# Attention: identity and causal masks of the mask products in float32r instead of bf16

## The chip, the cores and the metric

The kernel runs on one core of a Trainium2 chip. The core has a matrix engine (TensorE, PE in the rows), VectorE (DVE), ScalarE (ACT), GpSimd (POOL) and a queue of DMA issues (SyncE, SP). They run side by side and wait for each other by semaphores. The metric is the device time of one execution in microseconds (us), lower is better. A matrix product reads its two operands from the on-chip memory SBUF and adds up its result in PSUM. It has two parts: a weight load, which puts one operand into the array, and the matmul proper, which streams the columns of the other operand through it.

## What is computed

The reference is a transformer block with adaptive layer norm. The part that the change touches is a causal attention with 16 heads of 16 channels over 8 batches of 1024 tokens:

```python
h = _layernorm(x, axis=-1) * (1 + ca) + sa
att = jnp.einsum('bhtd,bhsd->bhts', q, k) * scale
causal = jnp.tril(jnp.ones((T, T), dtype=bool))
att = jnp.where(causal[None, None, :, :], att, -jnp.inf)
att = jax.nn.softmax(att, axis=-1)
y = jnp.einsum('bhts,bhsd->bhtd', att, v)
x = x + ga * (y @ Wp + bp)
```

Here q, k and v are projections of h. Behind it follow two layers of windowed attention and a gated MLP (another stage of the program), which the change leaves alone.

## The kernel before

Three stages follow each other: a small one for the modulation rows, the attention stage (`attention_stage`), and the layers' stage. Each begins when the one before has ended. The attention stage goes through the 8 batches ("turns"), and in each through 4 groups of 4 heads. A group is 12 steps (`STEPS1`): a step is one block of 128 keys against up to 512 queries. The instructions of each engine are written out in this order by Python loops; nothing reorders them afterwards.

Each group needs the scores twice. `first_pass` (L882) computes them with queries on the partitions, only for the row maxima, which VectorE takes (L1050). It makes 24 units of up to 512 keys for each group, two in each step. `scores` (L907) computes them with keys on the partitions and the maxima subtracted by two extra rows; ScalarE takes the exponentials from there (L728), and `meet_values` (L924) multiplies these by the values. Both kinds of scores handle a pair of heads at once: one head uses rows 0 to 63 of the array (48 or 50 of them), the other rows 64 to 127, each writing its own half of a PSUM slot of 1024 columns. There are three such slots (`a_ring`), filled in turn; a fill waits until ScalarE or VectorE has read the slot. Operands of the scores are float32r (the name `f32` in the rows covers both float32 and float32r).

Where a block lies on the diagonal, the forbidden pairs of query and key must be masked. `add_mask` does it with further products: the transposed "identity" picks 64 rows of a mask, and the product adds -1e30 to the forbidden scores in PSUM. The mask of 128 x 128 is made in two parts of 64 rows each, and each part is done for both heads, so one masked block takes four matmuls and four weight loads of 64 rows by 128 columns. With `mask_ts` (first pass) the two parts stream 128 and 64 columns, with `mask_st` (scores) 64 and 128. The mask matmuls belong to the same accumulation as the scores, and the last of them releases the slot to its reader.

In a group 16 of the 24 units and 16 of the 24 score blocks are masked. In these a block has 128, 256, 384 or 512 columns, each equally often. Over 32 groups that is 512 masked blocks of each kind.

The constants are made by GpSimd at the start of the stage: memsets to zero, then `affine_select`, which writes the fill value where a condition on row and column fails. A count on `const_made` orders them; TensorE and VectorE wait for its last value.

Of the kernel before, what the change touches and what calls it, by code (L numbers as in the profile page):

```python
# [18 lines left out]
F32R = mybir.dt.float32r  # L19
BF16 = mybir.dt.bfloat16  # L20
# [5 lines left out]
P = 128  # L26
# [105 lines left out]
class Chain(Signal):  # L132
# [5 lines left out]
    def step(self, ins):  # L138
        self.seen += 1
        ins.then_inc(self.sem, 1)  # L140
        self.eng.wait_ge(self.sem, self.at(self.i, self.seen))
# [208 lines left out]
def attention_stage(nc, sems, x_in, w_in, b_in, mod_dram, x1_dram, f_dram, parts_unused, max_unused, turns):  # L350

    with ExitStack() as ctx:
        sb = lambda name, shape, dt=F32: ctx.enter_context(nc.sbuf_tensor(name, shape, dt))
# [11 lines left out]
        b_p = sb("a_b_p", [P, C])  # L365
        gate_bp = sb("a_gate_bp", [P, 1, C])
        ident = sb("a_ident", [P, P])
        ident_h = sb("a_ident_h", [P, 2, P], BF16)
        mask_ts = sb("a_mask_ts", [P, 2, P], BF16)
        mask_st = sb("a_mask_st", [P, 2, P], BF16)  # L370
        mod_in = sb("a_mod_in", [P, 2, C])
        modb = sb("a_modb", [P, NMOD - 3, C])
        xl = sb("a_xl", [P, TB, C])
# [28 lines left out]
        const_made = plain("a_const_made")  # L402
# [198 lines left out]
        @block.gpsimd  # L601
        def _(pool):
            pool.memset(ident[:, :], 0.0).then_inc(const_made, 1)
            pool.memset(ident_h[:, :, :], 0.0).then_inc(const_made, 1)
            pool.memset(mask_ts[:, :, :], 0.0).then_inc(const_made, 1)
            pool.memset(mask_st[:, :, :], 0.0).then_inc(const_made, 1)
            pool.memset(v_t[:, :, :, D1:VW], 0.0).then_inc(const_made, 1)
            pool.wait_ge(const_made, 5)
            pool.memset(v_t[:, :, :, D1:D1 + 1], 1.0).then_inc(const_made, 1)
            pool.memset(mx[:, :, :, :, :, :], MASKED).then_inc(const_made, 1)  # L610
            for r in range(2):
                pool.wait_ge(const_made, 7 + r)
                pool.memset(k_st[64 * r + 32:64 * r + 64, :, :].bitcast(F32), -1.0).then_inc(const_made, 1)
            pool.wait_ge(const_made, 9)
            pool.affine_select(out=ident[:, :], in_=ident[:, :], compare_op=ALU.not_equal, fill=1.0, base=0,
                               pattern=[[-1, P]], channel_multiplier=1).then_inc(const_made, 1)

            for r in range(2):
                rows = slice(64 * r, 64 * r + 64)
                for m, op, fill, sign in ((ident_h, ALU.not_equal, 1.0, 1), (mask_ts, ALU.is_ge, MASKED, 1),  # L620
                                          (mask_st, ALU.is_ge, MASKED, -1)):
                    pool.wait_ge(const_made, 10 + 3 * r + (0 if m is ident_h else 1 if m is mask_ts else 2))
                    pool.affine_select(out=m[rows, :, :], in_=m[rows, :, :], compare_op=op, fill=fill, base=0,
                                       pattern=[[64 * sign, 2], [-sign, P]], channel_multiplier=sign)\
                        .then_inc(const_made, 1)
            pool.wait_ge(w_loaded, 16 * (NW + 4))

            def modulate(dst, src, name, shift, scale, scaling, scaled, done, a):

                aggr, rstd = norms[name]["aggr"], norms[name]["rstd"]  # L630
                pool.wait_ge(rstd_of[name].sem, rstd_of[name].at(a, 1))
                pool.sem_inc(scaling.sem, 1)
                for t in range(TB):
                    ins = pool.tensor_scalar(dst[:, t, :], src[:, t, :], aggr[:, t, 0:1], rstd[:, t:t + 1],
                                             ALU.subtract, ALU.mult)
                ins.then_inc(scaled.sem, 1)
                pool.wait_ge(scaled.sem, scaled.at(a, 1))
                pool.tensor_tensor(dst[:, :, :], dst[:, :, :], scale.broadcast_to([P, TB, C]), ALU.mult)\
                    .then_inc(scaled.sem, 1)
                pool.wait_ge(scaled.sem, scaled.at(a, 2))  # L640
                pool.tensor_tensor(dst[:, :, :], dst[:, :, :], shift.broadcast_to([P, TB, C]), ALU.add)\
                    .then_inc(done.sem, 1)

            def modulate_x(a):
                pool.wait_ge(mod_in_loaded.sem, mod_in_loaded.at(a, 1))
                modulate(xl, xl, "x", mod_in[:, 0:1, :], mod_in[:, 1:2, :], x_scaling, x_scaled, h_ready, a)

            pool.sem_inc(x_scaled.sem, 2)
            pool.sem_inc(x_scaling.sem, 1)
            modulate_x(1)  # L650

            def body(i, closing=False):
                pool_steps.start(pool, i)
                pool.wait_ge(mod_loaded.sem, mod_loaded.at(i, 1))
                pool.wait_ge(xr_loaded.sem, xr_loaded.at(i, 1))
                pool_steps.step(pool.tensor_tensor(gate_bp[:, 0, :], modb[:, 0, :], b_p[:, :], ALU.mult))
                pool.tensor_tensor(x1[:, :, :], x1[:, :, :], gate_bp[:, :, :].broadcast_to([P, TB, C]),
                                   ALU.add).then_inc(biased.sem, 1)
                if not closing:
                    modulate_x(i + 2)  # L660
                pool.wait_ge(biased.sem, biased.at(i, 1))
                for p in range(1 if closing else 2):
                    pool.wait_ge(gated.sem, gated.at(i, 2 * p + 2))
                    half = slice(4 * p, 4 * p + 4)
                    pool.tensor_tensor(x1[:, half, :], x1[:, half, :], f_t[:, half, :], ALU.add)\
                        .then_inc(x1_done.sem, 1)
                if closing:
                    rows, shape = f_t[:, END:TB, :], [P, TB - END, C]
                    pool.wait_ge(end_scaled, 1)
                    pool.tensor_tensor(rows, rows, modb[:, 2:3, :].broadcast_to(shape), ALU.mult)\  # L670
                        .then_inc(end_scaled, 1)
                    pool.wait_ge(end_scaled, 2)
                    pool.tensor_tensor(rows, rows, modb[:, 1:2, :].broadcast_to(shape), ALU.add).then_inc(end_done, 1)
                else:
                    modulate(f_t, x1, "f", modb[:, 1:2, :], modb[:, 2:3, :], f_scaling, f_scaled, f_done, i)
                pool_steps.end()

            for i in range(turns - 1):
                body(i)
            body(turns - 1, closing=True)  # L680
# [104 lines left out]

        @block.tensor
        def _(pe):
            pe.wait_ge(const_made, 16)
            pe.wait_ge(lo_split, 1)

            def program(mode, i):
# [191 lines left out]
        def _(dve):  # L983
            def program(mode, i):
# [120 lines left out]
                if mode == "lead":  # L1105
                    x_statistics(0)
                    dve.wait_ge(hi_split, 3)
                    dve.tensor_tensor(w_lo[:, :, :, :], w_raw, w_hi[:, :, :, :].bitcast(F32), ALU.subtract)\
                        .then_inc(lo_split, 1)
                    nearer("x", 0)  # L1110
                    dve.wait_ge(rstd_of["x"].sem, rstd_of["x"].at(0, 1))
                    step(normalise(xl, xl, "x", range(TB)))
                    dve.wait_ge(mod_in_loaded.sem, mod_in_loaded.at(0, 1))
                    step(dve.tensor_tensor(xl[:, :, :], xl[:, :, :], mod_in[:, 1:2, :].broadcast_to([P, TB, C]),
                                           ALU.mult))
                    dve.tensor_tensor(xl[:, :, :], xl[:, :, :], mod_in[:, 0:1, :].broadcast_to([P, TB, C]),
                                      ALU.add).then_inc(h_ready.sem, 1)
                    for c in range(CK):
                        low(("xT", c), xT_hi, 0)
                    for m in MATRICES:  # L1120
                        for half in range(2):
                            qk_low(("qk", m, half), 0)
                    dve.wait_ge(const_made, 16)
                    for q in range(4):
                        take_values(("v", q), 0)
                    for k in range(NUNIT):
                        reduce_unit(0, k, 0)
                        if k == NUNIT // 2:
                            x_statistics(1)
                        if k == NUNIT * 3 // 4:  # L1130
                            nearer("x", 1)
                    maxima(0, 0)
                    maxima_low(0, 0)
                    for k in range(PER_STEP * UNIT_LEAD):
                        reduce_unit(1, k, 0)
# [1224 lines left out]
```

## Time and profile before

| | |
|---|---|
| median of 3 runs | 4161.38 us (4150.5 to 4162.23) |
| profiled execution | 4156.13 us, span of its instructions 4154.3 us |
| TensorE busy | 3759.8 us, 91% of the span |
| VectorE, ScalarE, GpSimd busy | 3079.0, 2612.0, 1887.2 us |
| mean granted clock of TensorE | 0.964 of full speed |

TensorE's busy time counts matmuls from start to modelled end, and neighbours overlap, so 91% doesn't mean a full array. Distances between starts tell more than durations. A row of the timeline joins equal neighbours (x2, x4): its start is that of the first, its length reaches to the end of the last.

### The profile page before, as it was taken

How to read it: one execution, taken by the hardware profiler on the slowest of the kernel's cores; microseconds unless marked ns; L12 is line 12 of the kernel's file. 1: busy time of each engine (PE TensorE's matmuls, PEld its weight loads, DVE VectorE, ACT ScalarE, POOL GpSimd, SP SyncE). 2: the span in 40 equal slices, each digit the busy share in tenths (PEclk: the TensorE clock that was granted, in tenths of full speed). 3: DMA queues.
4: the chain of work that ended last, by engine and by line, in shares of the span. 5: the costliest groups of instructions: out<-in, count | busy, mean ns of one | idle time of the engine just before them, and what ended most of it. 6: DMA issues, size and time to landing. Idle time of an engine off the chain costs nothing.

```text
span 4154.3 us, 88049 instructions
## 1 busy us (share of the span) xinstructions
PE 3759.8 (91%) x33070; PEld 2895.4 (70%) x33070; DVE 3079.0 (74%) x7229; ACT 2612.0 (63%) x5759; POOL 1887.2 (45%) x1444
## 2 busy tenths in 40 slices
PE   4799999999998759999999999989999999999997
PEld 2354545445544347888888888878888888888886
DVE  4677777777776358777787877777888788788884
ACT  1355555555555447777777777767777777767774
POOL 1212322232233035555555555555666565656664
PEclk7799999999999879999999999999999999999999
DMA  4444244353441120000000000011000000000000
GB/s 124 88 74 119 58 112 102 73 125 75 92 128 34 33 67 31 15 20 18 17 20 15 20 17 18 17 43 41 22 28 27 23 26 22 26 24 25 24 23 21
DMA packets 146019, 195.93 MB, mean 47 GB/s; under 512 B 21596, under 2 KB 119608, under 8 KB 145600
## 3 DMA queue, kind: packets, MB, share of 16 engines
q1 hardware_dynamic: 145600, 190.31, 18.4%
q8 instruction: 267, 4.37, 0.5%
q14 instruction: 152, 1.25, 0.1%
HBM read 113.66 MB, written 67.16 MB: 44 GB/s over the span
## 4 chain that ended last, share of the span: by engine, by line
PE 24%; DVE 14%; ACT 12%; DMA 8%; issue 5%; POOL 0%; DVEq 0%; SPq 0%; POOLq 0%; ACTq 0%
PE b_bank_m L1914 10%; DMA b_hs<-b_fr 8%; PE b_bank_p L1914 5%; ACT b_e L1794 4%; DVE b_e L2142 3%; PE b_bank_et L1979 2%; PE b_bank_t L1914 2%; DVE b_qk_rot L2111 2%; ACT L1837 2%; DVE b_rot L2115 2%; PE b_bank_ot L1994 2%; PE b_bank_s L1968 1%; ACT b_e_t L1804 1%; DVE b_ag L2206 1%; ACT b_ag L1829 1%
## 5 line engine op out<-in xcount | busy, mean ns | idle before, releaser
L728 ACT ACTIVATE a_e_t<-a_ring 128x1024 f32<-128x1024 f32 (+3 forms) x768 | 610.9, 809 | 528.5 <-PE a_ring L869 371.7
L1050 DVE TENSOR_REDUCE a_mx<-a_ring 128x2 f32<-128x1024 f32 (+3 forms) x768 | 724.5, 956 | 233.8 <-PE a_ring L869 113.1
L1682 POOL TENSOR_TENSOR b_e<-b_e,b_share 128x512 f32<-128x512 f32 (+1 forms) x512 | 505.9, 991 | 801.2 <-DVE b_share L2150 801.1
L1794 ACT ACTIVATE b_e<-b_e,b_bias 128x256 f32<-128x256 f32 (+1 forms) x1024 | 494.2, 486 | 164.7 <-DVE b_bias L2142 163.8
L2142 DVE CUSTOM_DVE_ANT_0 b_e<-b_bank_s,b_mask,b_inv 128x256 f32<-128x256 f32 (+1 forms) x1024 | 415.8, 460 | 31.1 <-PE b_bank_s L1968 31.1
L1667 POOL TENSOR_TENSOR b_qk_rot<-b_qk_rot,b_rot 128x512 f32<-128x512 f32 x256 | 351.7, 1384 | 130.1 <-DVE b_rot L2115 130.1
L1804 ACT ACTIVATE b_e_t<-b_bank_et 128x512 f32<-128x512 f32 (+1 forms) x512 | 287.2, 561 | 184.2 <-PE b_bank_et L1979 184.1
L882 PE MATMUL a_ring<-a_k_st,a_q_st 48*128 48x512 f32 (+3 forms) x1536 | 328.2, 424 | 77.4 <-ACT a_e_t L728 41.6
L907 PE MATMUL a_ring<-a_q_st,a_k_st 50*128 50x512 f32 (+3 forms) x1536 | 340.0, 441 | 40.7 <-ACT a_e_t L728 13.7
L907 PEld LDWEIGHTS a_ring<-a_q_st,a_k_st 50*128 50x128 f32 x1536 | 147.5, 189 | 298.0 <-issue 145.0
L1979 PE MATMUL b_bank_et<-b_ident,b_e 128*128 128x128 f32 x1920 | 310.8, 282 | 43.1 <-ACT b_e_t L1804 43.1
L924 PE MATMUL a_outp<-a_e_t,a_v_t 128*32 128x512 f32 (+3 forms) x3072 | 338.6, 513 | 12.4 <-ACT a_e_t L728 7.2
L1979 PEld LDWEIGHTS b_bank_et<-b_ident,b_e 128*128 128x128 f32 x1920 | 216.9, 141 | 139.6 <-issue 113.2
L1914 PE MATMUL b_bank_m<-b_h_t_hi,b_w_hi 128*128 128x256 f32 x1024 | 295.1, 288 | 16.1 <-DVE b_ag L2223 12.7
L1914 PE MATMUL b_bank_m<-b_h_t_hi,b_w_lo 128*128 128x256 f32 x1024 | 286.8, 280 | 0.0
L1914 PE MATMUL b_bank_m<-b_h_t_lo,b_w_hi 128*128 128x256 f32 x1024 | 286.7, 280 | 0.0
L1994 PE MATMUL b_bank_ot<-b_e_t,b_v 128*64 128x128 f32 x3840 | 279.8, 283 | 0.0
L2111 DVE TENSOR_TENSOR b_qk_rot<-b_qk,b_tab 128x512 f32<-128x512 f32 x256 | 258.0, 1008 | 21.6 <-ACT b_qk L1763 7.2
L1701 POOL TENSOR_TENSOR b_hid_lo<-b_ag,b_hid_hi 128x768 fp32r<-128x768 f32 x128 | 236.6, 1848 | 71.2 <-ACT b_hid_hi L1843 71.2
L2115 DVE TENSOR_TENSOR b_rot<-b_qk,b_tab 128x512 f32<-128x512 f32 x256 | 247.8, 968 | 0.0
L882 PEld LDWEIGHTS a_ring<-a_k_st,a_q_st 48*128 48x128 f32 x1536 | 151.7, 194 | 130.6 <-ACT a_e_t L728 78.9
L1994 PEld LDWEIGHTS b_bank_ot<-b_e_t,b_v 128*64 128x64 f32 x3840 | 217.5, 137 | 32.9 <-issue 0.9
(238 smaller groups left out, 11010.3 us busy)
## 6 DMA issues: line engine op xcount, KB each, us to landing
a_q_st<-a_parts_q SPq DMA_DIRECT2D x192, 128.0 KB, 4.8
a_k_st<-a_parts_k SPq DMA_DIRECT2D x192, 128.0 KB, 7.5
a_parts_q<-a_qk_p SPq DMA_DIRECT2D x16, 1024.0 KB, 8.0
a_parts_k<-a_qk_p SPq DMA_DIRECT2D x16, 1024.0 KB, 8.1
b_fl<-f_rows SPq DMA_DIRECT2D x64, 256.0 KB, 4.1
a_xl<-in_L_attn_x SPq DMA_DIRECT2D x9, 1024.0 KB, 5.3
a_x<-in_L_attn_x SPq DMA_DIRECT2D x8, 1024.0 KB, 9.3
x_rows<-a_x SPq DMA_DIRECT2D x8, 1024.0 KB, 4.6
```

The costliest lines, as they stand in the source:

```text
L728: act.activation(e_t[:, step % 2, 2 * pair:2 * pair + 2, 0:cols], slot[:, :].rearrange("p (h t) -> p h t", h=2)[:, :, 0:cols], ACT.Exp).th ...
L882: mm = pe.matmul(slot[:, 512 * r:512 * r + cols], q_st[rows, 2 * g + pair, t * P:(t + 1) * P], k_st[rows, 2 * g + pair, 512 * piece:512 * ...
L907: mm = pe.matmul(slot[:, 512 * r:512 * r + cols], k_st[rows, 2 * g + pair, s * P:(s + 1) * P], q_st[rows, 2 * g + pair, lo:lo + cols], sta ...
L1050: dve.reduce_max(mx[:, g % 2, :, pair, piece, t:t + 1], slot[:, :].rearrange("p (r c) -> p r c", r=2)[:, :, 0:cols], AX.X)\
L1667: pool.tensor_tensor(qk_rot[:, a, :, :], qk_rot[:, a, :, :], rot[:, a, :, :], ALU.add)\
L1682: pool.tensor_tensor(weights, weights, share[:, h % SPS, 2 * j:2 * j + 2].unsqueeze(2) .broadcast_to([P, 2, 2 * WIN - lo]), ALU.mult).then ...
L1794: ins = act.activation(weights, weights, ACT.Exp, scale=-1.0, bias=bias[:, h % SPS, at:at + 1], accum_out=total[:, h % SPS, at:at + 1])
L1914: mm = pe.matmul(out, lhs(a), rhs(b), start=(first and j == 0), stop=(last and j == 2))
L1979: mm = pe.transpose(bank["et"][:, at:at + WIN], e[:, h % 2, j, hh, b * WIN:(b + 1) * WIN], ident[:, :])
L1994: mm = pe.matmul(bank["ot"][D2 * hh:D2 * (hh + 1), p * WIN:(p + 1) * WIN], v[:, u % 3, 2 * p + hh, :], e_t[:, j, 2 * hh + b, :], start=(b ...
L2111: dve.tensor_tensor(qk_rot[:, a, :, :], qk[:, a, :, :], cos, ALU.mult)
L2142: dve.tensor_tensor_reduce(out=e[:, h % 2, j, hh, lo:], in0=bank[f"s{hh}"][:, 2 * WIN * j + lo:2 * WIN * (j + 1)], in1=mask[:, int(w % NWI ...
```

## The change

The identity `ident_h` and both masks become float32r. GpSimd no longer clears the three tiles in place: it clears one float32 tile, `a_blank`, and the selects read from it and write the three float32r tiles. Two memsets fall away, so the counts of `const_made` are lower by two. The values are the same: 0, 1 and -1e30 up to rounding. `add_mask` itself is unchanged; its products read the new type. TensorE's, VectorE's and ScalarE's instructions keep their order and number.

```diff
--- before.py
+++ after.py
@@ -365,9 +365,10 @@
         b_p = sb("a_b_p", [P, C])
         gate_bp = sb("a_gate_bp", [P, 1, C])
         ident = sb("a_ident", [P, P])
-        ident_h = sb("a_ident_h", [P, 2, P], BF16)
-        mask_ts = sb("a_mask_ts", [P, 2, P], BF16)
-        mask_st = sb("a_mask_st", [P, 2, P], BF16)
+        blank = sb("a_blank", [P, 2, P])
+        ident_h = sb("a_ident_h", [P, 2, P], F32R)
+        mask_ts = sb("a_mask_ts", [P, 2, P], F32R)
+        mask_st = sb("a_mask_st", [P, 2, P], F32R)
         mod_in = sb("a_mod_in", [P, 2, C])
         modb = sb("a_modb", [P, NMOD - 3, C])
         xl = sb("a_xl", [P, TB, C])
@@ -601,17 +602,15 @@
         @block.gpsimd
         def _(pool):
             pool.memset(ident[:, :], 0.0).then_inc(const_made, 1)
-            pool.memset(ident_h[:, :, :], 0.0).then_inc(const_made, 1)
-            pool.memset(mask_ts[:, :, :], 0.0).then_inc(const_made, 1)
-            pool.memset(mask_st[:, :, :], 0.0).then_inc(const_made, 1)
+            pool.memset(blank[:, :, :], 0.0).then_inc(const_made, 1)
             pool.memset(v_t[:, :, :, D1:VW], 0.0).then_inc(const_made, 1)
-            pool.wait_ge(const_made, 5)
+            pool.wait_ge(const_made, 3)
             pool.memset(v_t[:, :, :, D1:D1 + 1], 1.0).then_inc(const_made, 1)
             pool.memset(mx[:, :, :, :, :, :], MASKED).then_inc(const_made, 1)
             for r in range(2):
-                pool.wait_ge(const_made, 7 + r)
+                pool.wait_ge(const_made, 5 + r)
                 pool.memset(k_st[64 * r + 32:64 * r + 64, :, :].bitcast(F32), -1.0).then_inc(const_made, 1)
-            pool.wait_ge(const_made, 9)
+            pool.wait_ge(const_made, 7)
             pool.affine_select(out=ident[:, :], in_=ident[:, :], compare_op=ALU.not_equal, fill=1.0, base=0,
                                pattern=[[-1, P]], channel_multiplier=1).then_inc(const_made, 1)
 
@@ -619,8 +618,8 @@
                 rows = slice(64 * r, 64 * r + 64)
                 for m, op, fill, sign in ((ident_h, ALU.not_equal, 1.0, 1), (mask_ts, ALU.is_ge, MASKED, 1),
                                           (mask_st, ALU.is_ge, MASKED, -1)):
-                    pool.wait_ge(const_made, 10 + 3 * r + (0 if m is ident_h else 1 if m is mask_ts else 2))
-                    pool.affine_select(out=m[rows, :, :], in_=m[rows, :, :], compare_op=op, fill=fill, base=0,
+                    pool.wait_ge(const_made, 8 + 3 * r + (0 if m is ident_h else 1 if m is mask_ts else 2))
+                    pool.affine_select(out=m[rows, :, :], in_=blank[rows, :, :], compare_op=op, fill=fill, base=0,
                                        pattern=[[64 * sign, 2], [-sign, P]], channel_multiplier=sign)\
                         .then_inc(const_made, 1)
             pool.wait_ge(w_loaded, 16 * (NW + 4))
@@ -785,7 +784,7 @@
 
         @block.tensor
         def _(pe):
-            pe.wait_ge(const_made, 16)
+            pe.wait_ge(const_made, 14)
             pe.wait_ge(lo_split, 1)
 
             def program(mode, i):
@@ -1120,7 +1119,7 @@
                     for m in MATRICES:
                         for half in range(2):
                             qk_low(("qk", m, half), 0)
-                    dve.wait_ge(const_made, 16)
+                    dve.wait_ge(const_made, 14)
                     for q in range(4):
                         take_values(("v", q), 0)
                     for k in range(NUNIT):
```

## Rows read from the trace of the kernel before

**Rows 1.** Part 1 of the page: engine, busy us, share of the span, instructions.

```profile
PE 3759.8 (91%) x33070; PEld 2895.4 (70%) x33070; DVE 3079.0 (74%) x7229; ACT 2612.0 (63%) x5759; POOL 1887.2 (45%) x1444
```

**Rows 2.** Windows: stretch, its us, busy us of each engine (instructions), clock, DMA.

```profile
90.00:158.00 68.00, 47.03 (x303) 22.78 (x301) 42.30 (x67) 12.11 (x18) 23.89 (x12) 0.50 0.63 119
158.00:1431.00 1273.00, 1149.65 (x11415) 618.74 (x11411) 891.14 (x1343) 691.44 (x959) 332.77 (x168) 0.97 0.38 87
...
495.00:498.90 3.90, 2.72 (x48) 1.70 (x44) 3.90 (x9) 1.36 (x3) 0.00 (x0) 1.00 0.64 216
498.90:505.80 6.90, 6.23 (x36) 4.21 (x37) 4.37 (x18) 3.34 (x6) 4.62 (x4) 0.51 0.11 36
1472.00:4154.00 2682.00, 2512.80 (x21120) 2217.50 (x21120) 2088.24 (x5718) 1891.79 (x4759) 1504.82 (x1238) 0.99 0.08 25
```

**Rows 3.** Waits of PE, 158 to 1431 us: in total, times, longest.

```profile
PE a_ring L882 <- ACT a_e_t L728: 41.6, 119, 0.7
...
PE a_ring L907 <- ACT a_e_t L728: 12.2, 21, 1.1
```

**Rows 4.** Groups by form: count, busy us, mean ns of one, idle time before.

```profile
L907 PEld LDWEIGHTS a_ring<-a_q_st,a_k_st 50*128 50x128 f32 x1536 | 147.5, 189 | 298.0 <-issue 145.0 <-DVE a_mx L1050 60.2 <-DVE a_qk_p L1029 40.2
...
L869 PE MATMUL a_ring<-a_mask_ts,a_ident_h 64*128 64x128 bf16 x1024 | 121.6, 234 | 0.0
...
L869 PEld LDWEIGHTS a_ring<-a_mask_ts,a_ident_h 64*128 64x128 bf16 x2048 | 61.4, 98 | 47.0 <-issue 31.5
```

**Rows 5.** Timeline of PE, 606.5 to 608.5 us: start, length of the row.

```profile
606.57 0.50 PE L907 MATMUL a_ring<-a_q_st,a_k_st 50*128 50x512 f32 x2
...
606.98 0.36 PE L882 MATMUL a_ring<-a_k_st,a_q_st 48*128 48x256 f32 x2
...
607.38 1.07 PE L924 MATMUL a_outp<-a_e_t,a_v_t 128*32 128x512 f32 x8
608.37 0.50 PE L907 MATMUL a_ring<-a_q_st,a_k_st 50*128 50x512 f32 x2
```

**Rows 6.** Timeline of the weight loads (PEld), 606.5 to 607.6 us.

```profile
606.57 0.19 PEld L907 LDWEIGHTS a_ring<-a_q_st,a_k_st 50*128 50x128 f32 x2
606.91 0.12 PEld L869 LDWEIGHTS a_ring<-a_mask_st,a_ident_h 64*128 64x128 bf16 x4 [0.15 <-issue]
606.96 0.19 PEld L882 LDWEIGHTS a_ring<-a_k_st,a_q_st 48*128 48x128 f32 x2
607.18 0.12 PEld L869 LDWEIGHTS a_ring<-a_mask_ts,a_ident_h 64*128 64x128 bf16 x4
```

**Rows 7.** Timeline of PEld, 498 to 499 us: blocks of 128 columns.

```profile
498.14 0.12 PEld L869 LDWEIGHTS a_ring<-a_mask_st,a_ident_h 64*128 64x128 bf16 x4
498.19 0.19 PEld L882 LDWEIGHTS a_ring<-a_k_st,a_q_st 48*128 48x128 f32 x2
498.36 0.12 PEld L869 LDWEIGHTS a_ring<-a_mask_ts,a_ident_h 64*128 64x128 bf16 x4
```

**Rows 8.** Timelines of PEld and PE, 728.6 to 729.3 us: unmasked blocks.

```profile
728.63 0.19 PEld L907 LDWEIGHTS a_ring<-a_q_st,a_k_st 50*128 50x128 f32 x2 [0.17 <-issue]
728.74 0.19 PEld L882 LDWEIGHTS a_ring<-a_k_st,a_q_st 48*128 48x128 f32 x2
...
728.98 0.40 PE L882 MATMUL a_ring<-a_k_st,a_q_st 48*128 48x512 f32 x2
729.21 0.39 PE L907 MATMUL a_ring<-a_q_st,a_k_st 50*128 50x512 f32 x2
```

**Rows 9.** Timeline of PEld, 493 to 493.3 us: `mask_ts`, then scores.

```profile
493.07 0.12 PEld L869 LDWEIGHTS a_ring<-a_mask_ts,a_ident_h 64*128 64x128 bf16 x4 [0.15 <-issue]
493.14 0.19 PEld L907 LDWEIGHTS a_ring<-a_q_st,a_k_st 50*128 50x128 f32 x2
```

**Rows 10.** Timeline of all engines, 47.5 to 53.3 us: end of the set-up.

```profile
47.78 0.41 POOL L623 TENSOR_SCALAR_AFFINE_SELECT a_mask_st<-a_mask_st 64x256 bf16<-64x256 bf16 x1
...
53.14 0.45 PE L811 MATMUL a_ring<-a_ident,a_xl 128*128 128x128 f32 x1 [36.57 <-DVE a_xl L1116]
```

## The prediction

> **What bounds the kernel now.** I read the windows first, stage by stage, because the change touches one stage only. The attention stage's steady part runs from 158 to 1431 us, and TensorE is busy 1149.65 of those 1273 us (90%), VectorE 891.14 and ScalarE 691.44 [rows 2]. The layers' stage begins only when the attention stage has ended, so what attention gains or loses goes whole into the end time. The page's first part says the same of the whole [rows 1].
>
> Then the waits of TensorE in that stretch: the longest entries are waits for ScalarE's exponentials (41.6 us in 119 waits) [rows 3]; the idle time in all is 1273 - 1150 = 123 us. So TensorE sets the pace, with small waits strewn between. One place is different: from 495 to 498.9 us VectorE is busy 3.90 of 3.90 us and TensorE 2.72 [rows 2]. There the blocks are 128 columns wide, and VectorE also takes the statistics of the finished rows.
>
> Then the groups of instructions: each form of mask product (64 or 128 columns, for `mask_ts` or `mask_st`) occurs 1024 times; one masked block takes four (two spans of columns, each in both row halves of the array), so there are 512 blocks with `mask_ts` and 512 with `mask_st`. Their weight loads show 98 ns each, those of the float32r scores 189 ns [rows 4]. Such a duration overlaps its neighbours, so it isn't the price; I take prices from the distances of starts in the timeline.
>
> **How the array runs there.** With the clock granted in full (2.4 GHz) a column takes 0.417 ns, so 64, 128, 256 and 512 columns take 0.027, 0.053, 0.107 and 0.213 us.
>
> A float32r load: from the start of the load of L882 at 606.96 to the next load at 607.18 are 0.22 us for 256 columns, from 606.57 to 606.91 0.34 us for 512 [rows 6], and from 498.19 to 498.36 0.17 us for 128 [rows 7]. Less the columns that leaves 0.113, 0.127 and 0.117 us. I take 0.11 us for the load and 0.01 for a gap behind the columns. The loads of both row halves start together (one row, x2) and are paid once.
>
> A bf16 load after float32r columns starts only when these have ended. Then it is short: from the first bf16 load to the float32r load of the next block are 0.05 us with `mask_st` (606.91 to 606.96, 498.14 to 498.19) [rows 6, 7] and 0.07 us with `mask_ts` (493.07 to 493.14) [rows 9]. This is both spans with all their loads; only the last span's columns still run.
>
> A float32r load after float32r columns is taken ahead: at 728.63 L907 begins its load, at 728.74 L882's load follows already, under L907's columns, and the next pair of matmuls starts 0.23 us after L882's at 728.98 [rows 8], which is 0.213 for the columns and 0.017 for the gap. The load is hidden there.
>
> **The change part by part.** No instruction is added on TensorE and none changes its place; only the type of operands changes, and with it the loads.
>
> *A block with `mask_st`.* Before, from the end of the block's columns to the first column of the next float32r block: gap 0.01, bf16 part 0.05, that block's load 0.11, in sum 0.17 us. After: the first mask load is taken ahead under the block's own columns, but the second can begin only when the first mask columns start (0.027 us long, so they hide little of it), and the next block's load only when the second start. So gap 0.01, load 0.11, load 0.11, in sum 0.23: +0.06 us. For a block of 128 columns the first mask load has only 0.053 us of cover and 0.06 of it shows: +0.12. The four widths come equally often: (3 x 0.06 + 0.12)/4 = 0.075 us, times 512 = 38 us.
>
> *A block with `mask_ts`.* Before 0.01 + 0.07 + 0.11 = 0.19, after 0.23: +0.04, and +0.10 at 128 columns. The mean is 0.055, times 512 = 28 us. Where values or a projection follow instead of scores (607.18 to 607.38 [rows 5, 6]), the array empties first, and the delay of the second span is the same 0.04.
>
> Together 66 us on TensorE's own path.
>
> *What takes some of it up.* A quarter of the blocks are 128 columns wide (256 blocks, on the mean 0.11 us each, 28 us), and these lie where VectorE is full [rows 2]: I let half of that vanish, -14. Of the waits of the scores for ScalarE, 119 + 21 [rows 3], each can give back 0.06 us, -8. A wait whose releaser is itself late by the mask gives nothing back, and most are of that kind, so I take no more. That leaves +44 us.
>
> *The set-up on GpSimd.* Three memsets become one and the selects write four bytes an element instead of two. The last select starts at 47.78 and takes 0.41 us, and TensorE starts its first transpose at 53.14, released by VectorE [rows 10]. The cover is 4.9 us. Even if all six selects doubled (6 x 0.4 = 2.4 us) nothing is late: 0. If that cover were gone, it would cost at most those 2.4 us.
>
> *Bounds.* Below: if a float32r load of this kind were wholly hidden, a block would take 0.01 + 0.027 + 0.053 = 0.09 instead of 0.17 or 0.19, and the sum would be 512 x (-0.08 - 0.10) = -92 us. [Rows 6, 7] show 0.11 us and more for a load with 50 or 48 rows, far more than the 0.03 to 0.05 us of mask columns, so I stay near the other end. Above: no load taken ahead, all three shown: 0.42 us a block, +0.25 and +0.23, in sum 246 us, some 200 after what the waits take up.
>
> The price of a load, once more: a bf16 pair of loads here costs about 0.02 us of the array (0.05 less the 0.027 of columns) [rows 6], a float32r pair 0.11. The Trainium skill (TensorE: Matmul & The Clock Gate, Weight-path perf modes) has the fast weight load for 128 weights whose type is not FP32, about twice as fast as measured there, and puts an ordinary load at columns/1.2 ns, 107 ns for 128 (section LDWEIGHTS). By it a bf16 load would be 53 ns and the change would cost an estimated 2 x 54 ns a block less what the columns cover. The trace agrees on the 107 and shows the bf16 loads as cheaper still.
>
> **The sum.** The profiled execution took 4156.13 us (span 4154.3): 4156 + 44 = 4200. The median of the runs is 4161.38, 5 us above it; for the median of the changed kernel I therefore say 4205 us. A measurement of this kernel can tell some 0.3%, about 12 us, from no change.
>
> **The rivals.**
>
> *Faster, by the clock.* The granted clock is 0.50 (1.2 GHz) from 90 to 158 us, and falls once more in most turns: in 495 to 498.9 TensorE is busy 70%, in 498.9 to 505.8 the clock is 0.51; over the steady part it is 0.97 [rows 2]. Half clock costs half of its time: 68 x 0.5 = 34 us at the start and 1273 x 0.03 x 2 x 0.5 = 38 us later, 72 in all. If longer loads made the engine count as busier and all of it came back, the end would be 4205 - 72 = 4133 us. It decides from 57 us on, four fifths of it. Against it: the array streams the same columns over a longer time. The Trainium skill (TensorE: Matmul & The Clock Gate, Part 1) has the clock follow how busy the engine is; by that a load that holds up the columns could count either way. 0.07. With 0.03 for loads that hide (the lower bound, 4069 us), faster has 0.10.
>
> *No difference.* The delay goes into TensorE's waits, 123 us of idle time to take up 66 [rows 2, 3]. It ends within 12 us of 4161. For it: the waits for ScalarE sit right behind masked blocks. Against it: the fills that ScalarE reads are late by the same masks. 0.10.
>
> *Slower by much more, loads not taken ahead.* Upper bound, 4161 + 200 = 4361. Against it: L882's load at 728.74 passes a whole pair of matmuls, both halves together [rows 8]. 0.08.
>
> *Slower, four passes.* A plain float32 product of 512 columns takes 0.99 us (607.38 to 608.37) where float32r takes 0.34 with its load [rows 5]. If the masks ran so, 128 columns would take 0.213 instead of hiding under a load of 0.11: +0.10 a block, 4205 + 102 = 4307. The float32r scores of 128 columns, 0.17 us with the load [rows 7], speak against it. The Trainium skill (FP8 and Floating Point Precision, TensorE Precision Notes) tells the reduced form, read once, from true FP32 in four passes. 0.04.
>
> *Slower, the clock falls more often.* If it fell in each of a turn's four head groups, 24 more falls of 6.9 us at half clock, 3 us each: 4205 + 72 = 4277. 0.08.
>
> My forecast, +15 to +90 us, has 0.60. Slower has 0.60 + 0.20 = 0.80, no difference 0.10, faster 0.10. The range 4160 to 4280 holds the forecast, the falling clock and half of the no-difference case, and leaves out the bounds at both ends.
>
> **What the changed profile would show.** Right: mask loads near 187 ns instead of 96; between the two spans 0.11 us instead of 0.04 to 0.07; the first mask matmul 0.01 to 0.02 us behind the scores' columns, with its load under them; a turn of 164 us longer by 5 to 6; columns of scores unchanged; the layers' stage 2682 us as before. Wrong: the mask load not before the end of the scores' columns (then nearer the upper bound), or loads of 64-row tiles with distances under 0.08 (then nearer none), or a clock of the steady part that moves from 0.97.

## The result and the profile after

The changed kernel takes 4218.71 us (median of 4 runs, 4205.62 to 4228.08), the kernel before 4155.94 us in the same session. The ratio is 1.0152, 95% interval 1.0115 to 1.0189: 63 us slower. The forecast was +44 us, slower, with a range of 4160 to 4280.

The page of the changed kernel, its busy times and the clock over 40 slices:

```profile
span 4226.1 us, 88047 instructions
...
PE 3867.4 (92%) x33070; PEld 3081.7 (73%) x33070; DVE 3080.7 (73%) x7229; ACT 2616.6 (62%) x5759; POOL 1886.2 (45%) x1442
...
PEclk6899979999999768999999999999999999999999
```

TensorE does as many matmuls as before and its weight loads are busy 186 us longer, 3081.7 against 2895.4 [rows 1]. The groups by form (same columns as [rows 4]) show where: each mask load now has a mean of 203 ns instead of 98.

```profile
L868 PEld LDWEIGHTS a_ring<-a_mask_st,a_ident_h 64*128 64x128 f32 x2048 | 190.2, 203 | 8.1
L868 PEld LDWEIGHTS a_ring<-a_mask_ts,a_ident_h 64*128 64x128 f32 x2048 | 189.6, 203 | 9.8
```

What they cost on the path stands in the timeline of the weight loads (from `add_mask` on, a line number is one lower than in the kernel before). First a score block of 512 columns, then one of 128:

```profile
555.15 0.19 PEld L906 LDWEIGHTS a_ring<-a_q_st,a_k_st 50*128 50x128 f32 x2 [0.52 <-DMA a_q_st<-a_m_part]
555.26 0.42 PEld L868 LDWEIGHTS a_ring<-a_mask_st,a_ident_h 64*128 64x128 f32 x4
555.60 0.19 PEld L881 LDWEIGHTS a_ring<-a_k_st,a_q_st 48*128 48x128 f32 x2
...
660.05 0.19 PEld L906 LDWEIGHTS a_ring<-a_q_st,a_k_st 50*128 50x128 f32 x2 [0.41 <-issue]
660.16 0.30 PEld L868 LDWEIGHTS a_ring<-a_mask_st,a_ident_h 64*128 64x128 f32 x4
660.38 0.19 PEld L881 LDWEIGHTS a_ring<-a_k_st,a_q_st 48*128 48x128 f32 x2
660.49 0.30 PEld L868 LDWEIGHTS a_ring<-a_mask_ts,a_ident_h 64*128 64x128 f32 x4
```

And the matmuls of the block of 512 columns:

```profile
555.16 0.49 PE L906 MATMUL a_ring<-a_q_st,a_k_st 50*128 50x512 f32 x2 [0.41 <-DMA a_q_st<-a_m_part]
555.49 0.33 PE L868 MATMUL a_ring<-a_mask_st,a_ident_h 64*128 64x64 f32 x4
555.66 0.44 PE L881 MATMUL a_ring<-a_k_st,a_q_st 48*128 48x512 f32 x2
```

From the load of L906 to the load of the next block at 555.60 are 0.45 us; before it was 606.57 to 606.96, 0.39 [rows 6]. That is the +0.06 of the forecast. The first mask load stands at 555.26, 0.11 behind L906's: it is taken ahead under the scores' columns, where the bf16 load had to wait for their end at 606.91. In the block of 128 columns (660.05) the loads stand at 0, 0.11, 0.33: two loads between 660.16 and 660.38, nothing to cover them. With bf16 the same distance from one load to the next block's was about 0.21 us (0.16 for load and columns, 0.05 for the masks, 498.14 to 498.19 [rows 7]), so +0.12.

These blocks are typical. Over all `mask_st` blocks that a first-pass block follows, at the full clock (102 to 120 in each width), the median of the same distance goes from 0.214 to 0.330 us for 128 columns, from 0.271 to 0.341 for 256, from 0.329 to 0.397 for 384 and from 0.392 to 0.454 for 512: +0.079 us in the mean of the four widths, where 0.075 was forecast. For `mask_ts` blocks with the values behind them (56 to 60 in each width) it is +0.094, +0.045, +0.043 and +0.039, mean 0.055, as forecast. By that the 512 blocks of each kind have 40 and 28 us of added path, some 8.6 us a turn.

Now the stage in pieces. A turn is taken from the first transpose of the attention's result `a_y` (L811 before, L810 after) in one batch to that in the next; such a stretch holds the same 1497 matmuls in both kernels. These are windows of the changed kernel (columns as in [rows 2]): a full turn, a stretch in the second full turn, the last turn, a stretch in that, and the layers' stage.

```profile
1169.80:1339.50 169.70, 158.60 (x1497) 102.21 (x1493) 119.89 (x182) 89.60 (x125) 47.57 (x24) 0.98 0.41 93
557.20:615.20 58.00, 57.70 (x351) 33.90 (x349) 30.70 (x54) 22.68 (x32) 11.60 (x8) 0.50 0.39 102
1339.50:1509.00 169.50, 146.02 (x1117) 83.19 (x1115) 70.19 (x106) 77.12 (x104) 28.74 (x14) 0.74 0.08 23
1390.10:1437.90 47.80, 44.96 (x261) 25.03 (x257) 20.95 (x24) 17.91 (x23) 5.73 (x3) 0.50 0.17 54
1545.20:4226.10 2680.90, 2510.09 (x21120) 2215.30 (x21120) 2087.43 (x5718) 1891.90 (x4759) 1504.78 (x1239) 0.99 0.08 25
```

And the same two turns of the kernel before:

```profile
1123.00:1287.00 164.00, 149.78 (x1497) 81.87 (x1493) 119.50 (x182) 89.11 (x125) 47.55 (x24) 0.98 0.42 96
1287.00:1435.50 148.50, 120.80 (x1118) 57.17 (x1116) 69.92 (x106) 76.71 (x104) 28.73 (x14) 0.87 0.09 26
```

At the same clock of 0.98 a full turn is 169.70 instead of 164.00 us. Of the six full turns five are longer by 27.0 us in all, 5.4 each. The other one (470.4 to 660.8) is longer by 26.8, because the clock stands at 0.50 from 557.2 to 615.2. The last turn is longer by 21.0, with a clock of 0.74 instead of 0.87. Before the first of these turns the changed kernel is 1.3 us quicker, and from the end of the last turn on 1.8 us, 0.2 of it lost before the layers' stage and 2.0 won in it. 27.0 + 26.8 + 21.0 - 1.3 - 1.8 = 71.7 us, which is the difference of the spans (4226.1 - 4154.3 = 71.8) up to rounding. The 1.3 us at the start hide the float32r loads of the first turn: the clock before it was at its lower level for less time in this execution, 106 us instead of 116.

So there are two parts: about 5.4 us a turn for the loads, which the forecast had (44/8 = 5.5), and some 20 us in the median, 30 in this execution (the longest of the four), for the clock, which it had only as a rival. The changed kernel was measured a second time, as a run of its own (below): +60 us, ratio 1.0158. Its profiled execution has no long stretch at the lower clock in the full turns, so the one at 557.2 isn't part of every execution.

What the waits took up can be read too, over six full turns of the kernel before (303 to 1287 us) and of that second run of the changed kernel (309 to 1329 us). TensorE's largest wait, in first-pass blocks for ScalarE's exponentials, falls from 33.7 us in 96 waits to 22.9 us in 48. All waits for ScalarE's exponentials together fall from 35.8 to 23.7 us, those for VectorE from 39.6 to 28.0, and TensorE's idle time from 84.6 to 60.7. That is 4.0 us a turn given back of the 8.6 added, 2.0 by ScalarE and 1.9 by VectorE. It leaves 4.6; the measured 5.95 a turn (984.2 to 1019.9 us) have a slightly lower clock in them, 0.97 instead of 0.98.

### The profile page after: what moved, and what is told of

The parts are those of the page before. It is cut to its first block, busy times and chain, and to the rows that moved or that the text cites. A ratio compares the mean times of both kernels' runs of the same rounds, so it can differ in the third digit from the quotient of the medians.

```text
span 4226.1 us, 88047 instructions
## 1 busy us (share of the span) xinstructions
PE 3867.4 (92%) x33070; PEld 3081.7 (73%) x33070; DVE 3080.7 (73%) x7229; ACT 2616.6 (62%) x5759; POOL 1886.2 (45%) x1442
## 4 chain that ended last, share of the span: by engine, by line
PE 24%; DVE 14%; ACT 12%; DMA 8%; issue 5%; POOL 1%; DVEq 0%; POOLq 0%; SPq 0%; ACTq 0%
PE b_bank_m L1913 10%; DMA b_hs<-b_fr 7%; PE b_bank_p L1913 5%; ACT b_e L1793 4%; DVE b_e L2141 3%; PE b_bank_et L1978 2%; DVE b_qk_rot L2110 2%; PE b_bank_t L1913 2%; ACT L1836 2%; DVE b_rot L2114 2%; PE b_bank_ot L1993 2%; ACT b_e_t L1803 1%; PE b_bank_s L1967 1%; DVE b_ag L2205 1%; ACT b_ag L1828 1%
## 5 line engine op out<-in xcount | busy, mean ns | idle before, releaser
L906 PE MATMUL a_ring<-a_q_st,a_k_st 50*128 50x512 f32 (+3 forms) x1536 | 351.6, 455 | 27.3 <-ACT a_e_t L727 11.7
L906 PEld LDWEIGHTS a_ring<-a_q_st,a_k_st 50*128 50x128 f32 x1536 | 152.8, 196 | 292.6 <-issue 169.7
L923 PE MATMUL a_outp<-a_e_t,a_v_t 128*32 128x512 f32 (+3 forms) x3072 | 352.7, 533 | 11.5 <-ACT a_e_t L727 6.5
```

The costliest lines, as they stand in the source:

```text
L906: mm = pe.matmul(slot[:, 512 * r:512 * r + cols], k_st[rows, 2 * g + pair, s * P:(s + 1) * P], q_st[rows, 2 * g + pair, lo:lo + cols], sta ...
L923: mm = pe.matmul(outp[32 * h:32 * h + VW, lo:512], v_t[:, s, 4 * g + h, :], e_t[:, (g * NSTEP + n) % 2, h, 0:512 - lo], start=(s == 0), st ...
```

## The experiments

All ratios are against the kernel before on the same chip, with the 95% interval.

**1. The changed kernel again.**

> The changed kernel once more, to see how far its time goes with the granted clock. Theory L (weight loads): about +43 us come from the masked blocks (the turns of 164 us are 5.3 us longer), the rest of the +63 us is time at half clock. Then the runs spread with their clocks: a run at 0.964 like before would stand near +43 to +48, one at 0.953 near +70, in between about 2.3 us for each 0.001 of clock. Rival C (the clock alone): the time follows the clock so closely that a run at the clock of before would show no more than +15. Rival P (path alone): +63 whatever the clock.

Measured: 4211.97 us, before 4152.21, ratio 1.0158 (1.0141 to 1.0175). Its profiled execution (span 4209.3, clock 0.958) has a full turn of 168.30 us and a last one of 160.10:

```profile
1160.70:1329.00 168.30, 157.20 (x1496) 100.89 (x1492) 119.85 (x182) 89.70 (x125) 47.66 (x24) 0.99 0.41 93
1329.00:1489.10 160.10, 136.41 (x1120) 77.07 (x1116) 70.02 (x106) 77.17 (x104) 28.76 (x14) 0.80 0.09 25
```

The four runs of the first session had clocks of 0.953, 0.954, 0.956 and 0.959, and spans of 4226.1, 4217.7, 4216.2 and 4203.7: the time follows the clock. With the four of this run (0.951 to 0.959, 4225.7 to 4207.8) a straight line through the eight has 2.6 us for each 0.001 and would be at 4194 at the clock of before (0.964), 40 us above its span. That is an extrapolation, since no execution of the changed kernel came that high. Where the two meet it holds: at 0.959 the changed kernel has spans of 4203.7 and 4207.8 us, and an execution of the kernel before at 0.959 (beside experiment 6, on another chip) has 4162.4, 41 to 45 less. Theory L holds, P falls, and C falls as an explanation of everything.

**2 and 3. One kind of mask alone.** Both kernels keep a bf16 identity and add a float32r one; `add_mask` takes the one of the mask's type. The edit against the changed kernel, for `mask_st` alone:

```diff
-        ident_h = sb("a_ident_h", [P, 2, P], F32R)
+        ident_h = sb("a_ident_h", [P, 2, P], BF16)
+        ident_r = sb("a_ident_r", [P, 2, P], F32R)
-        mask_ts = sb("a_mask_ts", [P, 2, P], F32R)
+        mask_ts = sb("a_mask_ts", [P, 2, P], BF16)
...
+                    ident_m = ident_h if mask is mask_ts else ident_r
```

> Only mask_st (the scores for ScalarE) is float32r, with a float32r identity of its own; mask_ts and its identity stay bf16. Theory L: 38 of the 66 us of TensorE's path, so +25 us after what the waits take up, +35 with its part of the clock; each block with mask_st 0.06 to 0.12 us longer, blocks with mask_ts as before. Rival S (what costs is a switch of type between neighbours): here the switches stay, at the other end of the block, and the cost is about that of the whole change or more, +60.

> Only mask_ts (the first pass for the maxima) is float32r. Theory L: 28 of the 66 us, so +18 us after the waits, +25 with its part of the clock; with the kernel that has only mask_st changed it adds up to the whole change (+63). Rival S: +60 or more, and the two don't add up.

Measured: `mask_st` alone 4201.7 us, ratio 1.0123 (1.0109 to 1.0138), +50 us. `mask_ts` alone 4184.41 us, ratio 1.0086 (1.0073 to 1.0099), +32 us. In sum 82, not 60 to 63. The windows of a full and the last turn, first of the kernel with `mask_st` changed:

```profile
308.70:475.90 167.20, 155.21 (x1497) 91.75 (x1493) 119.73 (x182) 89.67 (x125) 47.55 (x24) 0.98 0.40 93
1318.50:1483.00 164.50, 140.17 (x1120) 74.52 (x1116) 70.29 (x106) 77.01 (x104) 28.72 (x14) 0.76 0.09 24
```

and of the one with `mask_ts` changed:

```profile
304.90:470.80 165.90, 153.56 (x1494) 91.78 (x1492) 119.71 (x182) 89.22 (x125) 47.56 (x24) 0.98 0.40 95
1306.10:1464.30 158.20, 132.74 (x1117) 67.58 (x1115) 69.94 (x106) 76.90 (x104) 28.75 (x14) 0.79 0.08 25
```

At 0.98 of the clock the full turns are 3.2 and 1.9 us longer than 164.0, together 5.1. The forecast's shares were 38 and 28 of 66, that is 3.2 and 2.3 of 5.5 us. These are single turns, chosen for their clock; turns of these two kernels with more time at the lower clock take up to 169.8 and 167.3 us. At the same clock the loads add up: 5.1 against the 4.6 to 5.7 of the changed kernel's turns at 0.98. What doesn't is the clock: each kernel has the slow last turn (164.5 and 158.2 instead of 148.5), 16.0 and 9.7 us longer. Together that is 14 us more than in the second run of the whole change (160.1, 11.6 longer), and 5 more than in the first (169.5). Rival S, a price on each switch of type, would give full turns as long as the whole change's, and they aren't.

**4. The set-up alone.** The code of the changed kernel with all three tiles bf16.

> Only the set-up part of the change: one float32 blank tile that the selects read, two memsets fewer, but the three tiles are bf16 as before. Theory L: 0 us (within 12), since TensorE starts 4.9 us after the last select. A rival would be that the set-up moves the start of TensorE and with it the granted clock of the first 150 us: up to 10 us either way.

Measured: 4151.85 us, ratio 1.0005 (0.9995 to 1.0015). Nothing, as forecast.

**5. float32r in the last turn only.** Both sets of tiles exist; the edit in `add_mask`:

```diff
+                    ident_m = ident_h
+                    if mode == "closing":
+                        ident_m, mask = ident_r, mask_ts_r if mask is mask_ts else mask_st_r
```

> Both types of identity and masks are in SBUF; the float32r ones are used only in the last turn (the part of the program without a next turn), bf16 in the seven before. The last turn has 48 masked score blocks and some 27 masked first-pass blocks. Theory L alone (loads): 48 x 0.079 + 27 x 0.055 = 5 us of TensorE's path, +3 to +5 us. Theory L+C (loads, and the clock that then falls earlier in the thinly filled last turn, where time at half clock rose from 39 to between 65 and 88 us in the kernels with float32r masks): +10 to +20 us.

Measured: 4173.23 us, ratio 1.0052 (1.0038 to 1.0067), +23 us, for 7% of the change (72 of the 1024 masked blocks; those of the last turn's first 31 us are still bf16). Its windows: a full turn (bf16), the last turn, and a stretch in it.

```profile
961.20:1125.90 164.70, 151.10 (x1494) 82.96 (x1492) 119.67 (x182) 89.07 (x125) 47.64 (x24) 0.97 0.42 95
1290.40:1456.60 166.20, 141.50 (x1120) 78.16 (x1116) 70.19 (x106) 77.03 (x104) 28.76 (x14) 0.77 0.08 24
1341.40:1385.80 44.40, 42.14 (x239) 23.18 (x239) 18.83 (x22) 15.73 (x21) 3.97 (x3) 0.50 0.18 58
```

The last turn is 17.7 us longer than before, of which the loads are 3 to 5 by the forecast. From 1341.4 on the clock is at its lower level for 44 us; over the whole turn a mean clock of 0.77 instead of 0.87 means about 77 us at the lower level instead of 39. So the clock's part is real, and here it lies in this turn. There the first pass of the next batch is missing and TensorE is filled less: busy 120.80 of 148.50 us before, 81%, against 91% in a full turn.

**6. float32r everywhere but in the last turn** (the condition turned round).

> The complement of the kernel with float32r masks in the last turn: float32r in the first seven turns, bf16 in the last. Theory L+C: seven turns of 5 us more, +35 to +42 us (one or two early falls of the clock in the body among them), and the last turn back at 146 to 150 us with some 40 us at half clock; together with the +22 us of its complement it gives the whole change. Rival E (the clock at the end depends on what the body did before): the last turn stays at 158 us or more.

Measured: 4204.27 us, ratio 1.0128 (1.0106 to 1.0150), +48 us, and rival E was right: the last turn, now with bf16 masks, takes 158.40 us.

```profile
1155.00:1323.20 168.20, 157.20 (x1496) 100.96 (x1492) 119.82 (x182) 89.68 (x125) 47.66 (x24) 0.99 0.40 94
1323.20:1481.60 158.40, 133.24 (x1119) 64.00 (x1115) 69.97 (x106) 77.01 (x104) 28.76 (x14) 0.78 0.08 24
1357.00:1404.90 47.90, 42.93 (x255) 17.47 (x253) 20.74 (x27) 17.53 (x23) 18.70 (x10) 0.50 0.00 1
```

The clock falls at 1357, 34 us into the turn, a few us after the last float32r masks, and stays low for 48 us. In the kernel before it falls at the same place, 34.6 us into its last turn, but is back after 6.8 us, as two windows of it show (it falls once more at 1335.2, again for 6.8 us):

```profile
1321.50:1328.40 6.90, 5.58 (x30) 2.31 (x28) 2.75 (x3) 2.46 (x4) 6.90 (x7) 0.51 0.01 2
1328.40:1335.20 6.80, 5.28 (x72) 2.96 (x72) 4.05 (x7) 2.72 (x6) 6.64 (x4) 1.00 0.00 1
```

I can't say from these runs what decides between the two. The two halves of the change, 23 and 48 us, come to 71 and not to 60 or 63, as with the two masks.

**7 and 8. Wider mask columns.** The first span of `mask_st` streams 128 columns instead of 64, the added ones zero. The edit is the same in the changed kernel and in the one before:

```diff
-                        mm = add_mask(slot, 0, mask_st, ((0, 64), (0, P)))
+                        mm = add_mask(slot, 0, mask_st, ((0, P), (0, P)))
```

> The changed kernel, but the first of the two spans of mask_st streams 128 columns instead of 64 (the added half of the mask is zero). Theory L: these columns run under the load of the next weights (0.11 us), so the turns stay at 168.5 to 170.5 us, 0 us (within 12) from the changed kernel, +62 from before. Rival F (columns are on the path): 512 x 0.027 = 14 us of path, +9 more. Rival C: with more columns streamed the clock falls less, and the time is up to 15 us under the changed kernel's.

> The kernel before (bf16) with the same wider first span of mask_st. Theory L: bf16 loads take no time on the path, so here the columns count: 512 x 0.027 = 14 us of path, +9 us after the waits. If it is 0, the bf16 loads, not the columns, set the length of the masks' part.

Measured: in the changed kernel 4200.65 us, ratio 1.0105 (1.0086 to 1.0125); in the bf16 kernel 4158.86 us, ratio 1.0014 (1.0003 to 1.0025), +8 us by the medians, +6 by the ratio. The changed kernel's turns with the wider span:

```profile
1156.00:1325.70 169.70, 158.71 (x1497) 102.34 (x1493) 119.88 (x182) 89.77 (x125) 47.65 (x24) 0.98 0.40 93
1325.70:1481.70 156.00, 131.56 (x1117) 75.81 (x1115) 70.00 (x106) 77.00 (x104) 28.76 (x14) 0.84 0.09 25
```

A full turn is 169.70 us as without the wider span: the added columns run under the next load, as theory L says; with bf16 they show, with 6 to 8 us where 9 were expected. What is gained, 11 to 18 us against the two medians of the changed kernel, is the last turn (156.0 us at a clock of 0.84). Two executions of this kernel reach the clock of before, 0.964 and 0.965, with spans of 4187.9 and 4188.2 us, 34 us above that of before, of which the wider span can be at most 8: float32r masks are slower without any loss of clock.

**9. The wider span in the last turn of the changed kernel alone.**

> The changed kernel, with the wider first span of mask_st (128 columns instead of 64, zeros added) in the last turn alone: 48 score blocks. Theory C: the gain that the wide span gave everywhere (20 us against the changed kernel) was the clock of the last turn, so it comes here too: the last turn at 156 to 160 us, +45 to +52 us against before. Rival R (that gain was scatter of the clock from one run to the next): like the changed kernel, +63.

Measured: 4208.8 us, ratio 1.0129 (1.0106 to 1.0152), runs from 4195 to 4217.5. The profiled execution, the fastest of the five, has the short last turn (155.70 us, clock 0.84); the median lies between the two theories, and its interval overlaps both that of the changed kernel and that of the wide span everywhere. Inconclusive.

**10 and 11. The masks one block later.** The masks of a score block are multiplied after the columns of the first-pass block that follows. The core of the edit:

```diff
                     if diagonal:
-                        mm = add_mask(slot, 0, mask_st, ((0, 64), (0, P)))
-                    mm.then_inc(filled.sem, 1)
+                        due.append((slot, filled))
+                    else:
+                        mm.then_inc(filled.sem, 1)
...
+                def masks_due():
+                    while due:
+                        slot, filled = due.pop()
+                        add_mask(slot, 0, mask_st, ((0, 64), (0, P))).then_inc(filled.sem, 1)
```

`masks_due` is called in `first_pass` behind the columns, and once more behind each group of first-pass blocks in case none followed.

> The kernel before (bf16) in another order: the masks of a score block are multiplied after the columns of the first-pass block that follows, just ahead of that one's own masks. Theory L: the first-pass block's float32r weights are now loaded under the score block's columns, and one shown load of 0.11 us goes away in each of the 512 pairs: -56 us of path. The exponentials start later by the first-pass block's columns (0.05 to 0.21 us), which gives some back: -25 to -40 us. Rival W (the waits for ScalarE take it all): within 12 of before.

> The changed kernel (float32r) in the order that cost the bf16 kernel 99 us: the masks of a score block behind the columns of the next first-pass block. Theory L: with bf16 the order hid one load of 0.11 us in each pair and still lost, by waits for ScalarE that it made later; with float32r masks every mask load is as long as the one hidden, so nothing is won back: the loads of four mask spans follow each other, 0.08 us more a pair than the change costs in the old order. 99 + 63 + 30 = +170 to +200 us against before. If it is +120 or less, the waits take the loads up.

Measured: with bf16 4249.67 us, ratio 1.0240 (1.0208 to 1.0273), +99 us where I expected -25 to -40; with float32r 4382.38 us, ratio 1.0554 (1.0527 to 1.0581), +227 where I expected 170 to 200. The weight loads of the bf16 kernel in this order:

```profile
602.31 0.19 PEld L915 LDWEIGHTS a_ring<-a_q_st,a_k_st 50*128 50x128 f32 x2 [0.84 <-issue]
602.41 0.19 PEld L889 LDWEIGHTS a_ring<-a_k_st,a_q_st 48*128 48x128 f32 x2
602.83 0.12 PEld L869 LDWEIGHTS a_ring<-a_mask_st,a_ident_h 64*128 64x128 bf16 x4 [0.23 <-issue]
602.88 0.15 PEld L869 LDWEIGHTS a_ring<-a_mask_ts,a_ident_h 64*128 64x128 bf16 x4
602.99 0.19 PEld L915 LDWEIGHTS a_ring<-a_q_st,a_k_st 50*128 50x128 f32 x2
```

The load at 602.41 is hidden, as meant. But TensorE's longest wait (in total, times, longest; 333 to 1313 us) is

```profile
PE a_ring L889 <- ACT a_e_t L728: 75.7, 138, 0.9
```

against this in the same stretch of the kernel before:

```profile
PE a_ring L882 <- ACT a_e_t L728: 33.4, 95, 0.7
```

In some six turns this wait grew by 42 us, 7 a turn, and a full turn at a clock of 0.97 takes 171.10 us (the others, at a lower clock, 174). Rival W wasn't strong enough: the waits took more than all. The float32r kernel in this order has turns like this, with the clock at 0.86:

```profile
1101.70:1296.30 194.60, 178.68 (x1495) 112.51 (x1493) 120.96 (x182) 91.37 (x125) 47.56 (x24) 0.86 0.36 81
```

Most of what it loses beyond the bf16 kernel in this order is clock: a mean of 0.86 over 194.6 us means some 54 us of each turn at the lower level, against 10 of 171.1.

**12. No mask products.** The kernel before without any; the softmax inside diagonal blocks then sees later tokens too.

> The kernel before with all mask products left out (the attention is then not causal inside the diagonal blocks), for what the bf16 masks cost in all. Theory L: a masked block's 0.17 or 0.19 us between its columns and the next load shrinks to the gap of 0.01 to 0.02, since the next float32r load is taken ahead: 512 x (0.155 + 0.175) = 169 us of path, and as ScalarE and VectorE then wait less and hold TensorE up more, 100 to 130 us of it in the end time. Rival: only the columns count (512 x 2 x 0.08 = 82 us of path), -50 to -60 us.

Measured: 4164.64 us, ratio 1.0021 (1.0005 to 1.0038), +9 us where both theories expected a gain. Two of its full turns:

```profile
1130.80:1288.40 157.60, 135.59 (x982) 67.87 (x980) 118.60 (x182) 89.02 (x124) 47.60 (x24) 0.98 0.43 99
963.70:1130.80 167.10, 147.70 (x983) 71.68 (x981) 118.84 (x182) 89.17 (x125) 47.60 (x24) 0.89 0.42 94
```

At a clock of 0.98 the turn is 6.4 us shorter than 164.0. TensorE's busy time falls by 14.2 us (149.78 to 135.59), less than the 169/8 = 21 that I had reckoned, and 7.8 of these 14.2 come back as idle time. The clock, 0.89 in the second window and much the same in three more of the six full turns, takes the 6.4 us back. So of the path that this change added some 60% counted. Of the 21 us that I reckoned for leaving the masks out 6.4 count at the same clock, and in the time of the whole kernel none.

## Why the prediction was right

- **The load's price** (0.11 us), from distances of starts and not from the 98 and 189 ns of the groups: right. 0.45 against 0.39 us for a block of 512 columns, +0.12 for one of 128, loads 0.11 apart, and +0.079 and +0.055 in the means of the two kinds where 0.075 and 0.055 were forecast.
- **The first mask load taken ahead**: right, 555.15 to 555.26, and the first mask matmul at 555.49 stands 0.01 us behind the scores' columns (555.16 + 0.11 + 0.213). Only the duration of a load was off, 203 ns instead of 187, and the path doesn't pay by it.
- **The shares of the two masks**: 3.2 and 1.9 us a turn by single changes, forecast 3.2 and 2.3 before the waits took some up.
- **Two thirds reach the end time**: right in the sum. Some 8.6 us of path were added a turn (forecast 66/8 = 8.2) and 4.6 to 5.7 at the same clock were measured (forecast 5.5). The split was another: 8 of the 66 us were to come back from ScalarE's waits, 1.0 a turn, and 2.0 did; 14 from VectorE's, 1.75 a turn, and 1.9 did. The prediction had no row for the half that it let vanish in the narrow blocks, so the agreement of this term is in part luck.
- **The set-up**: right, no difference, shown by its own run.
- **The columns of the masks under the loads**: right; doubling half of them left the turn at 169.70.
- **The term that was mis-sized** is the clock. I had it at nothing in the sum and as a rival with 0.08 and +72 us, as more falls of 6.9 us each. It came not so but as longer stretches at the lower level (58.0 and 47.8 us in the profiled execution, 27 and 41 in that of the second run). That the change brings them is shown: the eight executions of the changed kernel have clocks of 0.951 to 0.959, the 17 of the kernel before beside the second run 0.963 to 0.968 (0.959 to 0.967 beside the later experiments). They account for about 20 us in the median; with some 43 for the loads (8 turns of 5.4) that makes the +63. The steady part's clock went from 0.97 to 0.94 in the profiled execution, which the prediction had named as a sign of being wrong. What starts and ends such a stretch stays open. Without this term the sum was 19 us short, and the range, which took in this rival up to 4277, held the result.

The rivals on the other side fell: no load was hidden behind another's few columns, the clock gave nothing back, and the masks didn't run in four passes: from the first mask matmul to the next block's columns are 0.17 us (555.49 to 555.66), and the block's 64 and 128 mask columns would take 0.32 us four times over.

## What to carry to other kernels

Price a weight load by the distance between starts, not by its duration, and ask what streams while it runs: in this kernel a float32r load of 0.11 us is free behind float32r blocks of 256 columns (0.341 us for the block, against 0.330 with 128) and shows behind 64. A small product that is slipped between large ones should therefore have the cheap (bf16) load, even if its neighbours are float32r. Before counting on time saved on TensorE, look at its waits and at its clock: here all mask products were left out and the time was no shorter.

## What the runs showed of the hardware beyond that

The clock stayed at its lower level although TensorE had work all the time: 57.70 us busy in 58.00 us (557.2 to 615.2), at 0.50. Just before the fall it was busy at the full clock:

```profile
540.00:557.20 17.20, 16.15 (x167) 10.90 (x165) 11.12 (x15) 8.99 (x14) 0.00 (x0) 1.00 0.57 112
```

The same products in other turns ran at the full clock. The Trainium skill (TensorE: Matmul & The Clock Gate, Why this matters for your kernels) advises against idle gaps between bursts of matmuls, so that throughput doesn't drop in mid-kernel; from 474 us to the end of this stretch TensorE's longest idle gap is 0.8 us, so the advice doesn't explain this fall.

Without the masks the clock was 0.89 in most turns (0.98 with them), and with zero columns added under a load it was 0.84 in the last turn (0.74 to 0.80 without). I don't know the cause: the inconclusive run and the bf16 last turn behind float32r turns leave open what starts and ends a long stretch.

Float32r loads are taken ahead under running float32r columns (555.26, 602.41). A bf16 load behind float32r columns never was in the rows I read (606.91, 493.07, 602.83), nor in the medians over the `mask_st` blocks of the kernel before: there the first mask load begins 0.166, 0.225, 0.281 and 0.340 us behind the scores' load for 128 to 512 columns, which is the load and the columns, while in the changed kernel it begins after 0.109 us at every width.
